# Smaller PSUM pieces for an attention with 16 narrow heads: four banks in turn for ScalarE, single banks for the row maxima, products by one tile, scaling and biases on GpSimd

## The reference, cut to what matters

```
x = hidden_states                                  # [8, 1024, 256]
n = layernorm(x)
q, k, v = n @ wq + bq, n @ wk, n @ wv + bv         # 16 heads of 16
q, k = rope(q, k)   # in bf16, on the last 256 tokens of each sequence
scores = q @ k^T / 4                               # [8, 16, 1024, 1024]
x = x + (softmax(scores) @ v) @ wo + bo
x = x + experts_and_shared_mlp(layernorm(x))       # not touched
```

## Time and profile before

| | |
|---|---|
| three runs | 2601.09 us median, 2585.87 to 2603.83 |
| profiled execution | 2598.11 us, its span 2596.3 us, mean granted PE clock 0.966 |
| busy in the span | PE 91%, PEld 52%, DVE 73%, ACT 63%, POOL 30% |
| attention | from 0 to about 1710 us: head until 57.9, 12 steps of maxima alone until 92.5, 512 steps until 1669.9, tail |
| experts and shared MLP | the rest, about 886 us, the same code in both kernels |

### The profile page before, as it was taken

How to read it: one execution, slowest core, us unless ns; L and a number is a source line. 1 busy time by engine, 2 the same in 40 slices (tenths; PEclk the granted TensorE clock), 3 DMA queues, 4 the chain that set the end, 5 groups by cost and what they waited for, 6 DMA issues and landing times. The chain is left out here.

```text
span 2596.3 us, 41961 instructions
## 1 busy us (share of the span) xinstructions
PE 2371.4 (91%) x16142; PEld 1350.2 (52%) x16142; DVE 1891.8 (73%) x2545; ACT 1637.4 (63%) x3104; POOL 787.6 (30%) x987
## 2 busy tenths in 40 slices
PE   6799999999999989999988988879997999999997
PEld 4233333333333333333333332378886888888886
DVE  4888988987987898898898889356565455555553
ACT  2588888887887887887887888632232343333332
POOL 2031241241251142143043022000001466666664
PEclk9799999999999999999999999889999999999998
DMA  1010010010010011010001001042232344544453
GB/s 53 1 34 1 1 54 13 1 59 8 1 34 33 1 33 34 1 33 33 1 17 33 1 17 33 12 143 80 90 97 62 99 106 107 113 102 90 107 110 37
DMA packets 104208, 122.47 MB, mean 47 GB/s; under 512 B 7538, under 2 KB 91251, under 8 KB 104051
## 3 DMA queue, kind: packets, MB, share of 16 engines
q1 hardware_dynamic: 79474, 86.76, 10.6%
q0 software_dynamic: 24576, 33.57, 7.6%
HBM read 78.37 MB, written 41.94 MB: 46 GB/s over the span
## 5 line engine op out<-in xcount | busy, mean ns | idle before, releaser
L450 DVE TENSOR_REDUCE sb_MX<-ring 128x2 f32<-128x1024 f32 x1024 | 1222.9, 1219 | 241.6 <-PE ring L773 233.7
L591 ACT ACTIVATE sb_PR<-rot 128x512 f32<-128x512 f32 x2048 | 1112.5, 608 | 179.7 <-PE rot L786 171.7
L786 PE MATMUL rot<-sb_QT,sb_KT 32*128 32x512 bf16 x2048 | 558.8, 392 | 54.8 <-ACT sb_PR L591 33.2
L797 PE MATMUL pv<-sb_PR,sb_VA 128*32 128x512 f32 x4096 | 557.1, 617 | 0.5
L773 PE MATMUL ring<-sb_KT,sb_QT 32*128 32x512 bf16 x2048 | 398.1, 394 | 76.2 <-DVE sb_MX L450 73.0
L773 PEld LDWEIGHTS ring<-sb_KT,sb_QT 32*128 32x128 bf16 x2048 | 96.0, 91 | 577.5 <-DVE sb_MX L450 335.4
L310 POOL CAST sb_QP<-sb_MX 128x16 bf16<-128x16 f32 x64 | 16.3, 255 | 924.8 <-DVE sb_MX L456 924.8
L1086 ACT ACTIVATE ex_GL<-ex_gu 128x512 f32<-128x512 f32 x128 | 76.5, 597 | 347.6 <-PE ex_gu L63 234.4
L1153 DVE TENSOR_TENSOR ex_HF<-ex_GL,ex_gu 128x512 f32<-128x512 f32 x128 | 87.5, 684 | 250.9 <-ACT ex_GL L1086 237.3
L786 PEld LDWEIGHTS rot<-sb_QT,sb_KT 32*128 32x128 bf16 x2048 | 142.5, 91 | 208.7 <-ACT sb_PR L591 190.8
L1050 POOL DMA_INDIRECT out<-ex_YS,ex_rows_out x128 | 208.9, 1632 | 44.1 <-issue 43.7
(11 more groups left out here) (172 smaller groups left out, 4163.2 us busy)
## 6 DMA issues: line engine op xcount, KB each, us to landing
sb_XA<-x SPq DMA_DIRECT2D x8, 1024.0 KB, 6.4
sb_XR<-x SPq DMA_DIRECT2D x8, 1024.0 KB, 5.3
out<-sb_XR SPq DMA_DIRECT2D x8, 1024.0 KB, 8.7
xn<-sb_XN SPq DMA_DIRECT2D x8, 1024.0 KB, 4.5
sh_XG<-xn SPq DMA_DIRECT2D x16, 512.0 KB, 5.5
sh_X<-out SPq DMA_DIRECT2D x16, 512.0 KB, 5.1
weights<-WgT SPq DMA_DIRECT2D x16, 512.0 KB, 3.7
weights<-WuT SPq DMA_DIRECT2D x16, 512.0 KB, 4.7
```

Of the source, the lines that this page charges most:

```text
L450: nc.vector.reduce_max(MX[:, unit % 2, half, 2 * pair:2 * pair + 2, qt % 4], ring[m % 2][:], AX.X).then_inc(ring_done, 1)
L591: out = nc.scalar.activation(PR[V % P_STEPS][:, j, :], R[:], ACT.Exp, scale=0.25)
L786: nc.tensor.matmul(R[:], KT[g][r, P * kt:P * kt + P], QT[g][r, 512 * qh:512 * qh + 512], start=True, stop=True, tile_position=(r.start, 0) ...
L797: out = nc.tensor.matmul(pv_bank[head(j), :], VA[b % 2][:, kt, 4 * g + j, :], PR[V % P_STEPS][:, j, :], start=(kt == 0), stop=(kt == TT - 1))
```

## The change

It has five parts.

1. **Banks.** `ROT` becomes 4. The maxima get `RING = 3` single banks in place of two double ones, so `score_rows` makes one head by 512 keys, with a wait of its own, and `maximum` reduces one bank; there are now four of each in a step, `m` to `m + 3`.
2. **Products** come one tile of 128 tokens and 256 columns at a time: `qk` is split in `q` and `k`, and `v` and `proj` go from 4 double pieces to 8 single ones per batch. The table beside the steps is laid out anew, `ot` is fixed at `S % 8 == 3`.
3. **The bias of q** is no longer two matmuls with a row of ones. ScalarE copies q to `QS`, and GpSimd adds `b_q` into `QP` (`bias_q`).
4. **The scaling** of a unit's output moves to GpSimd (`scale`); VectorE keeps the reciprocal.
5. **GpSimd** follows the steps and works in pieces: `add_bias` four times 512 columns, `normalise` four times 512, `add_projection` 8 times 256.

```diff
-    ROT = 3
+    ROT = 4
+    RING = 3
...
-        unit, n = m // 16, m % 16
-        c = (2, 0, 3, 1)[n % 4]
-        return unit, c // 2, c % 2, 4 * (unit % 2) + n // 4
+        unit, n = m // 32, m % 32
+        return unit, (2, 3, 0, 1)[n % 4], n // 4 % 2, 4 * (unit % 2) + n // 8
...
-        ring = [ctx.enter_context(nc.psum_tensor(f"ring{i}", [P, 2, 512], F32)) for i in range(2)]
+        ring = [ctx.enter_context(nc.psum_tensor(f"ring{i}", [P, 512], F32)) for i in range(RING)]
...
+            def bias_q(b, i):
+                pool.wait_ge(rot_done, done(("q", b, i)))
+                n = TILES.index(i)
+                out = QP[b % 2][:, i, :, 0:HD]
+                nc.gpsimd.tensor_tensor(out, QS[n % 2][:].rearrange("p (h c) -> p h c", c=HD),
+                                        b_q[:].rearrange("p (h c) -> p h c", c=HD), ALU.add).then_inc(q_biased, 1)
...
-            def add_bias(b):
+            def add_bias(b, n):
                 pool.wait_ge(xr_in, 16 * (b + 1))
-                nc.gpsimd.tensor_tensor(XR[:], XR[:], b_o[:].unsqueeze(1).to_broadcast([P, TT, H]),
-                                        ALU.add).then_inc(bias_ready, 1)
+                x = XR[:, 2 * n:2 * n + 2, :]
+                nc.gpsimd.tensor_tensor(x, x, b_o[:].unsqueeze(1).to_broadcast([P, 2, H]), ALU.add).then_inc(bias_ready, 1)
...
+            def scale(unit):
+                b, g, qh = unit // UNITS, unit % UNITS // 2, unit % 2
+                pool.wait_ge(recip_ready, unit + 1)
+                nc.gpsimd.tensor_tensor(
+                    AO[:, 4 * qh:4 * qh + 4, 64 * g:64 * g + 64].rearrange("p t (j c) -> p t j c", c=HD),
+                    AR[:, :, 0:HD].rearrange("p (t j) c -> p t j c", j=4),
+                    RD[:].rearrange("p (t j) -> p t j", j=4).unsqueeze(3).to_broadcast([P, 4, 4, HD]),
+                    ALU.mult).then_inc(ao_ready, 1)
...
+            for V in range(LAST):
+                b, S = V // STEPS, V % STEPS
+                more = b < B - 1
+                if S % 8 == 4 and 8 * b + S // 8 + 1 < UNITS * B:
+                    split_maxima(8 * b + S // 8 + 1)
+                if S % 8 == 5 and V >= 13:
+                    scale((V - 13) // 8)
+                for item in beside(V):
+                    if item[0] == "proj":
+                        add_projection(b - 1, item[2])
+                    elif item[0] == "aot":
+                        split(item, AH, AL, as_ready)
+                    elif item[0] == "xt":
+                        split(item, XH, XL, xs_ready)
+                    elif item[0] == "q":
+                        bias_q(b + 1, item[2])
+                if more and b and S == 10:
+                    clear_maxima(b + 1)
+                if more and 13 <= S <= 16:
+                    normalise(0, b + 2, XA, XA, xn_ready, S - 13)
+                if more and S == 29:
+                    rope(b + 1)
+                if b and 33 <= S <= 36:
+                    normalise(1, b, XN2, XR, xn2_ready, S - 33)
+                if b and 47 <= S <= 50:
+                    add_bias(b, S - 47)
...
-                nc.vector.reduce_max(MX[:, unit % 2, half, 2 * pair:2 * pair + 2, qt % 4], ring[m % 2][:], AX.X
+                nc.vector.reduce_max(MX[:, unit % 2, half, j, qt % 4:qt % 4 + 1], ring[m % RING][:], AX.X
                                      ).then_inc(ring_done, 1)
...
-                own.inc(nc.vector.reciprocal(RD[:], AR[:, :, HD]))
-                own.wait(dve)
-                nc.vector.tensor_tensor(
-                    AO[:, 4 * qh:4 * qh + 4, 64 * g:64 * g + 64].rearrange("p t (j c) -> p t j c", c=HD),
+                nc.vector.reciprocal(RD[:], AR[:, :, HD]).then_inc(recip_ready, 1)
...
-                if m >= 2:
-                    pe.wait_ge(ring_done, m - 1)
-                for n in range(2):
-                    r = head(2 * pair + n)
-                    out = nc.tensor.matmul(ring[m % 2][:, n, :], QT[g][r, P * qt:P * qt + P],
-                                           KT[g][r, 512 * half:512 * half + 512], start=True, stop=True,
-                                           tile_position=(r.start, 0))
-                out.then_inc(ring_full, 1)
+                if m >= RING:
+                    pe.wait_ge(ring_done, m - RING + 1)
+                r = head(j)
+                nc.tensor.matmul(ring[m % RING][:], QT[g][r, P * qt:P * qt + P], KT[g][r, 512 * half:512 * half + 512],
+                                 start=True, stop=True, tile_position=(r.start, 0)).then_inc(ring_full, 1)
...
-        26: ("qk", 1, 6), 27: ("ot", 2), 28: ("qk", 1, 7), 30: ("q2", 4), 31: ("qk", 1, 0), 33: ("qk", 1, 1),
+              20: (1, "xt", 1, 0), 21: (1, "xt", 0, 1), 22: (0, "q2", 3), 23: (1, "xt", 1, 1), 24: (1, "q", 6), 25: (1, "k", 6),
+              26: (1, "q", 7), 27: (1, "k", 7), 28: (1, "q", 0), 29: (1, "k", 0), 30: (0, "q2", 4), 31: (1, "q", 1),
```

More of the change, by code:

```diff
@@ L99, in beside @@
     def beside(V):
         b, S = V // STEPS, V % STEPS
-        item = (BESIDE if b >= 0 else BESIDE_FIRST).get(S)
-        if item is None:
-            return []
-        if item[0] in ("q2", "ot"):
-            unit = UNITS * b + item[1] - (UNITS if item == ("ot", 7) else 0)
-            return [(item[0], unit)] if 0 <= unit < UNITS * B else []
-        return [(item[0], b + item[1], *item[2:])] if 0 <= b + item[1] < B else []
-    HEAD = ([("xt", 0, h, half) for half in range(2) for h in range(KH)] + [("qk", 0, i) for i in (6, 7, 0, 1, 2, 3, 4, 5)]
+        out = []
@@ L111, in attention @@
+        if V >= 11 and S % 8 == 3:
+            unit = (V - 11) // 8
+            out.append(("ot", unit // UNITS, unit % UNITS))
+        table = BESIDE if V >= 0 else FIRST
+        if S in table:
+            more, kind, *rest = table[S]
+            if 0 <= b + more < B:
+                out.append((kind, b + more, *rest))
+        return out
+    HEAD = ([("xt", 0, h, half) for half in range(2) for h in range(KH)]
+            + [(n, 0, i) for i in TILES for n in ("q", "k")]
             + [("qT", 0, 0, 0), ("qT", 0, 0, 1), ("bo",)])
-    TAIL = ([("ot", UNITS * B - 1)] + [("aot", B - 1, h, half) for half in range(2) for h in range(KH)]
-            + [("proj", B - 1, i) for i in range(4)] + [("x2t", B - 1, h, half) for half in range(2) for h in range(KH)]
+    TAIL = ([("ot", B - 1, UNITS - 1)] + [("aot", B - 1, h, half) for half in range(2) for h in range(KH)]
+            + [("proj", B - 1, i) for i in range(TT)] + [("x2t", B - 1, h, half) for half in range(2) for h in range(KH)]
@@ L144, in attention @@
         bv = sb("bv", [P, KH, P], F32)
-        bq_in = sb("bq_in", [1, H], F32)
-        bq = sb("bq", [1, 2, H], FR)
-        one = sb("one", [1, P], FR)
+        b_q = sb("b_q", [P, H], F32)
+        QS = [sb(f"QS{n}", [P, H], F32) for n in range(2)]
         cs_in = sb("cs_in", [P, 2, ROPE_TILES, HD], F32)
@@ L168, in attention @@
         W_raw = AO[:].rearrange("p a c -> p (a c)").rearrange("p (k n) -> p k n", k=KH)
-        PJ = [sb(f"PJ{n}", [P, 2, H], F32) for n in range(2)]
+        PJ = [sb(f"PJ{n}", [P, H], F32) for n in range(4)]
         LG = sb("LG", [P, TT, E], F32)
@@ L355, in _ @@
             pool.wait_ge(const_ready, 1)
-            rope(0)
+            for i in TILES:
+                bias_q(0, i)
+                if i == TILES[1]:
+                    rope(0)
             pool.wait_ge(rot_done, done(("bo",)))
-            own.inc(nc.gpsimd.tensor_tensor(b_o[:], b_o[:], PJ[0][:, 0, :], ALU.add))
-            own.wait(pool)
+            nc.gpsimd.tensor_tensor(b_o[:], b_o[:], PJ[0][:], ALU.add).then_inc(bo_ready, 1)
+            pool.wait_ge(bo_ready, 1)
+            for n in range(TT // 2):
+                add_bias(0, n)
@@ L658, in _ @@
                     empty(item)
[L659 removed]
+                if V >= STEPS and V % STEPS == 51:
                     gate_powers(V // STEPS - 1)
```

236 lines of the change are left out of this document (98 added, 138 removed), and 14 rows, old and new, of the table BESIDE.

## The result

The changed kernel takes 2428.65 us (median of four runs, 2426.78 to 2429.26). The kernel before, run beside it on the same chip, takes 2600.44. The ratio is 0.9346, with a 95% interval of 0.9315 to 0.9377. The profiled execution took 2429.04 us, its span is 2427.3 at a mean granted clock of 0.974. The forecast was 2450, in a range of 2410 to 2540.

What follows compares the result with a forecast made beforehand. It took order and buffers as the bound: ScalarE's loop, plus a stop in five batches. A batch of 159 + 10.4 + 11.0, say 181, gave -145, the head -7: 2601 - 152 = 2449, taken as 2450, range 2410 to 2540.

Steps and rivals of the forecast that it cites:

- ScalarE's loop: Attention step, PV to PV through ScalarE's exponentials: four banks leave one exponential in the chain, 2.92 to 2.44 us.
- Reductions: VectorE's maxima over 512 columns: starts 0.61 us apart, 0.69 long, taken from another instruction's row; 0.56 the lower bound.
- Ring's loop: Three single banks for maxima, VectorE's reductions and TensorE waiting on each other: steps go at 2.48 us at best.
- The product's step: TensorE's attention step with a single product piece: 1.65 + 0.81 = 2.46 us, lengthening none of the 32 steps.
- VectorE's other work: VectorE's work between reductions, without the scaling: all 10.4 us per batch charged as lengthening the steps.
- Irregular steps: Steps with transposed result and piece 4.6, gate logits 2.3, copies of pv 2.8, S = 24 1.3: 11.0 us per batch.
- The stop: TensorE's halt at S = 37 to 39, VectorE's scaling held by GpSimd's add: 6.8 us in five batches, to go.
- GpSimd: GpSimd's load per batch: 57 us busy plus 10 for scalings and biases, hidden unless GpSimd falls behind.
- Head: The stretch before the batches: q-and-k tiles with half the columns per pass save 8, less 1 for GpSimd's rotation: -7.
- The fixed part of a reduction: Rival: each 512-column reduction blocks VectorE for 0.69, a step 2.76; 2590 us, no change; chance 0.05.
- Score matmuls side by side: Rival: separate waits stop score matmuls on TensorE running together, a group 0.86 for 0.32; about 2770 us; chance 0.05.
- GpSimd was late: Rival: GpSimd, strictly in order, delays TensorE, each of eight maxima one step late; 2608 us, no change; chance 0.04.

Runs made afterwards that it cites:

- experiment 4: The kernel before the change with only the residual's bias cut into four GpSimd instructions of 512 columns: 2569.93 us, ratio 0.9907.
- experiment 2: The changed kernel with the residual's bias in one GpSimd instruction over 2048 columns at S = 44, scaling still on GpSimd: 2428.35 us.
- experiment 7: The changed kernel with the scaling back on VectorE, all of GpSimd's pieces kept: 2465.36 us.
- experiment 1: The changed kernel with three banks in turn for ScalarE in place of four, one bank unused: 2576.67 us, ratio to before 0.9959.
- experiment 8: The changed kernel with the table beside the steps laid out anew, GpSimd's rotation and the gate work moved with it: 2414.96 us.
- experiment 11: The new table of experiment 8 with two entries exchanged, the first gate logits from S = 49 to 45, a transpose from 45 to 49: 2415.3 us.
- experiment 5: The changed kernel with reductions reading only the first 256 of 512 columns, leaving half the keys out of each maximum: 2360.09 us, ratio 0.9127.
- experiment 6: The changed kernel with q and k of a tile again in one product of 512 columns, four banks kept: 2455.14 us.
- experiment 9: The kernel before with only the new banks (four for ScalarE, three single ones for the maxima, reductions of 512): 2575.38 us, ratio 0.9955.
- experiment 10: The changed kernel with the eighth bank given to the maxima: four single banks there, three in turn for ScalarE: 2550.55 us.
- experiment 3: The changed kernel with the residual's bias in one GpSimd instruction at S = 44 and the scaling back on VectorE: 2485.21 us.

## Why the prediction was right

**ScalarE's loop** ("2.92 - 0.48 = 2.44"): shown from both sides. With three banks a plain step is 2.94, with four and an idle VectorE 2.45, and the eighth bank given to the maxima leaves it at 2.94. Whether the 2.45 is the loop or ScalarE's five items of 0.49 isn't told apart.

**Reductions** ("I take 0.61"): back to back they start 0.60 us apart by the median and last 0.68 each. The price came from a row of another instruction and held within 2%. By the 120 cycles of the Trainium skill ("VectorE: DVE Perf Modes", TRN2 errata) one would be 0.658 by estimate. The measured distance is 0.06 under that and the duration 0.02 over it.

**Ring's loop** ("2.48"): 2.49 where nothing else binds.

**The product's step** ("1.65 + 0.81 = 2.46 ... just under the loop"): this step of the prediction was off. It is 2.55 and lies over the loop. I halved a piece of 1.63, but a piece has a fixed part: its passes go 0.12 apart, the last takes 0.32 until the next matmul is out (5 x 0.12 + 0.32 = 0.91 with the rounding). If all 32 such steps showed it, it would be 2.2 us per batch; only ten stand at 2.55 with nothing longer beside, 0.7.

**VectorE's other work** ("I charge all 10.4"): too much. Halving the reductions frees far more than 10.4 us of VectorE in a batch, and the batch gains 7.0.

**Irregular steps** ("11.0"). The prediction counts from one PV to the next; so do the numbers here, as means over the batches 2 to 6. The gate logits (3.54 each against 3.61), S = 24 (3.76, 1.3 over the loop as foreseen) and the eight steps with the transposed result (4.7 over the loop together against 4.6; 2.94 to 2.96 in six of them) came as worked out. The copies of `pv` were mis-sized: the steps with one and those behind them lie 5.5 over the loop together, against 2.8, and 4.1 of this falls on the four pairs with a long transpose (qT) in one of the two. So these terms are 13.6 in place of 11.0, and all else over 64 x 2.48 is 7.0 in place of 10.4: 179.3 in place of 180.4. The sum came out nearer than its terms. The steps of 2.17 from exponential to exponential (S = 5, 10, 16, 18, 34, 58) give nothing back: there only the first exponential before them comes late, and from PV to PV no step is under 2.49.

**The stop** ("6.8"): 6.0 by experiment 4. Which part removes it was left open in the prediction, which named two; experiment 2 shows that moving the scaling is enough. In the kernel before, pieces are enough too.

**Scaling**: charged at 7.4 a batch; experiment 7 has 4.8 to 5.8.

**GpSimd**: 69.7 us a batch against 57 + 10 foreseen. One of the signs of being wrong was that TensorE waits for GpSimd. In batch 4 it does so once for more than a quarter of a microsecond, at S = 24, where the sum had it:

```profile
861.27 1.26 POOL L340 TENSOR_TENSOR sb_XL<-sb_XT,sb_XH 128x512 fp32r<-128x512 f32 x1
...
862.65 0.19 PEld L61 LDWEIGHTS rot<-sb_WH,sb_XH 128*128 128x128 f32 x1 [1.01 <-ACT sb_PR L606]
```

The profile names ScalarE, but the exponential that frees this bank, the first of the step, was done at about 861; the split ended at 862.53. Another sign, more waiting of TensorE for VectorE than for ScalarE, did not come: in the batches 1 to 6 the idle time put down to VectorE is 414 us, but 322 of it are the 0.84 behind each PV, and the 92 left stand against 128 for ScalarE.

**Head** ("-7"): -12.0. The low clock of the earlier trace rows was read off the passes; the profile has no granted clock below 1.00 for that stretch (24 to 57.6), but its passes of 512 columns go 0.43 apart, against 0.27 in the earlier trace rows. Two terms were off, with opposite signs. ScalarE stood 5.17 us for the bias of q, where I had put 1, as the rotation stood ahead of the third one on GpSimd. And from 28.4 to 38.6 us the passes went 0.12 apart instead of 0.21, at the upper level of the clock (columns of the windows as above):

```profile
16.00:28.40 12.40, 7.28 (x36) 7.07 (x35) 7.36 (x16) 3.42 (x7) 0.78 (x2) 0.72 0.30 85
28.40:38.60 10.20, 7.03 (x59) 6.83 (x59) 0.00 (x0) 3.16 (x9) 9.71 (x13) 1.00 0.00 0
```

```profile
36.46 3.47 POOL L347 TENSOR_TENSOR sb_QP<-sb_QS,sb_b_q 128x256 bf16<-128x256 f32 x5
37.27 0.37 ACT L621 COPY sb_QS<-rot 128x256 f32<-128x256 f32 x1 [5.17 <-POOL sb_QP L347]
```

**Batches in all** ("-145"): -163.5. Of the 18 us between, 12 are the six full batches (179.3 against 181.3) and 7 the last batch, where I had scaled 186.4 by 0.928 to 173.0 and it took 165.8. In the kernel before that batch ran at a granted clock of 0.94, now at 1.00.

**Steps of maxima and the tail** (left "as they are"): 2.1 and 4.4 longer. In the tail the granted clock of the changed kernel is 0.50 from 1513 to 1547 us, and the time follows it: 930.6 to 931.3 us behind the last exponential where the profile has this unbroken low stretch and a short one before it (the changed kernel, experiments 1, 2, 8 and 11), 925.1 to 926.7 where it is broken up (the kernel before, experiments 5, 6, 9 and 10); experiments 3, 4 and 7 lie between. Why it is broken up in some isn't shown. The sums were off by -18.5 (batches), -5.0 (head) and +6.5 (what was left as it is); part of the nearness of the forecast is that these have opposite signs.

**The rivals.** The fixed part of a reduction is hidden (0.60 apart). Score matmuls side by side were lost in part: in about half of the steps of a batch one matmul for a maximum goes behind its partner, by 0.25 to 0.6 us and once by 1.25 (batch 4), mostly behind transposes or other work of VectorE. Steps with a transpose still hold 2.49, so it is the ring's loop that shows there and no added cost. GpSimd was late in the head and for the split at S = 24, and in batch 4 for nothing else.

**What the parts are worth** is not a sum. Taken out of the changed kernel one at a time, the fourth bank costs 148 us, the scaling 37, the split of q and k 27, the pieces of the bias 0; put into the kernel before, the banks alone bring 12, by the ratio 0.9955. Banks and single pieces work together: with three banks a step waits for two exponentials with a single piece and without one (2.94), with double pieces each heavy step is TensorE's whatever the banks. Between experiment 9 (197.2 a batch) and the changed kernel (179.3) lie 18 us; 4.8 for the scaling, 3.8 for q and k and about 2 for the stop (experiment 3 against 7), each measured in the changed kernel, leave some 7, for the double v and projection pieces, the bias matmuls and the old table. These weren't taken apart.

## What to carry to other kernels

Count the uses of a rotating buffer within one step before giving it a bank: with five uses a step, three banks put two exponentials on the loop and four banks one, worth 0.5 us of 2.9, while the same bank given to the other ring left such a step at 2.94. A step that is bounded by several loops at nearly the same level (2.45, 2.49, 2.55 here) moves only when all of them are lowered, so a change of one may measure as next to nothing (the banks alone: 0.9955) and still be half of the gain. When a piece is cut in two, take the fixed part of a piece from the rows (here 0.2 us), and don't halve it.
